# Last layer: the weights' low halves made by VectorE in thirds instead of by GpSimd in one piece

## The chip, the cores and the metric

One core of one Trainium2 chip runs the whole program. The metric is the time of one execution in microseconds (us) of device time. The engines are named as the profile names them: PE is TensorE (PEld its weight load), DVE is VectorE, ACT is ScalarE, POOL is GpSimd and SP is SyncE, which here only issues DMAs.

## The reference

Four layers follow each other on 8 x 512 tokens of 128 features. Only the last one is touched:

```python
x = x + layernorm(L1_ffn(layernorm(x)))

def L1_ffn(hidden, gate_W, w1_e, w3_e, w2_e, w1_s, w3_s, w2_s):    # 4096 tokens, 8 experts, F = 512
    probs = softmax(flat @ gate_W.T)
    top_v, top_i = top_k(probs, 2)
    gates = zeros(T, 8).at[arange(T)[:, None], top_i].set(top_v)
    g = silu(einsum('td,edf->etf', flat, w1_e))
    u = einsum('td,edf->etf', flat, w3_e)
    out_e = einsum('etf,efd->etd', g * u, w2_e)
    routed = einsum('te,etd->td', gates, out_e)
    shared = (the same silu(x w1_s) * (x w3_s) w2_s, summed over 8 slices of 64 features) / 8
    return 0.5 * shared + 0.5 * routed
```

Every token goes through the shared expert and through the two experts that the gate picked.

## The kernel before

The layer works in tiles of 512 tokens: 8 tiles of the shared expert first, then 23 tiles of routed tokens, which were scattered to DRAM by expert and are loaded one tile at a time. `TILES` lists the 31 tiles, and `uses[i]` is the weight set of tile i. The shared tiles use one set; every routed tile has its own set of three matrices (gate, up, down), each 128 x 512, loaded as one buffer `raw` of 128 x 3 x 512.

Products are made to near full precision from two halves: a number a is cut into a high half (fp32r, a copy rounded by ACT) and a low half a - high, and `mm3` (L108 to L110) adds three matmuls, high x high, high x low and low x high. So three kinds of operand are cut: the tokens of a tile (`xh`, `xl`), the weights (`wh`, `wl`) and the gated products of each step (`hh`, `hl`).

A tile has four steps c = 0 to 3, one for each 128 of the 512 hidden features; steps are counted through as m. In step m:

- PE: `up(m)`, three matmuls into a bank of `sw_g` and three into a bank of `sw_u`; then `down(m - 3)`, three into `sw_d`. At c = 0 it then turns the finished tile i - 2 back (`turn_out`, 4 transposes), at c = 1 it turns the next routed tile's tokens (`turn_in`, 4 transposes). `up` at c = 0 first waits until the tile's weights and tokens are cut: `wh_ready`, `wl_ready`, `xh_ready`, `xl_ready`. PE issues in this order alone, so what it waits for at `up` holds everything behind it.
- ACT: `gated(m)` (silu), `high_half(m - 1)` (`sw_hh`), at c = 1 `finish(i - 2)` (four `sw_yo` pieces), at c = 2 `token_high(i + 1)` (`sw_xh`), and at c = 0 `cut_high` of the next tile's weights (`sw_wh`, one instruction of 1536 columns).
- DVE: `product(m)` (`sw_hf`), `low_half(m - 1)` (`sw_hl`), at c = 2 `token_low(i + 1)` (`sw_xl`) behind these two, at c = 3 `fetch(i - 1)` (`sw_dT`).
- POOL: once a tile `cut_low` (`sw_wl`, 1536 columns) and `send(i - 2)`, four indirect stores of 128 tokens each into `sw_ys`. Before that, in the shared tiles, it issues 64 indirect stores that scatter the tokens (`scatter`).
- SP: loads of weights (two `raw` buffers, so a load waits until the set two before has been cut low) and of tokens (`xin`, five buffers).

The order on each engine is the order in which the code is written; nothing reorders it, and engines meet only at semaphores. For the first routed tile `turn_in` comes at c = 3, not at c = 1, so that the scatter can end first.

Of the kernel before, what the change touches and what calls it, by code (L numbers as in the profile page):

```python
# [6 lines left out]
F32 = mybir.dt.float32  # L7
# [3 lines left out]
ALU = mybir.AluOpType  # L11
ACT = mybir.ActivationFunctionType
# [9 lines left out]
FC = F // P  # L22
# [2482 lines left out]
def routed_layer(nc, X, ident, w, consts, out, padded):  # L2505
# [5 lines left out]
    XR, YR, RING, LAG, WR = 5, 3, 4, 3, 3  # L2511
    TILES = [("shared", b) for b in range(FRONT)] + [("routed", j) for j in range(NT)] + [("shared", b) for b in range(FRONT, B)]
    N = len(TILES)
# [8 lines left out]
    with ctx:  # L2522
# [73 lines left out]
        @block.sync  # L2596
        def _(sp):
            def load_weights(s, expert):
                if s >= 2:
                    sp.wait_ge(wl_ready, s - 1)  # L2600
                sp.dma_start(raw[s % 2][:], w["all"][expert]).then_inc(w_loaded[s % 2], 16)

            def store(b):
                sp.wait_ge(done, b + 1)
                sp.dma_start(out[b].rearrange("(t p) d -> p t d", p=P), X[:, b * T:(b + 1) * T, :]).then_inc(out_stored, 16)

            for dst, src in first_loads:
                sp.dma_start(dst, src).then_inc(first_loaded, 16)
            load_weights(0, NE)
            sp.dma_start(ids[:], consts["ids"]).then_inc(ids_loaded, 16)  # L2610
            for dst, src in table_loads:
                sp.dma_start(dst, src).then_inc(tables_loaded, 16)
            sp.wait_ge(where_ready, 1)
            for j in range(NT):
                expert = sp.value_load(where[0:1, 0, j:j + 1], min_val=0, max_val=NE - 1)
                load_weights(j + 1, expert)
                if j == 0:
                    sp.wait_ge(scattered, 16 * 2 * B * T)
                if j >= XR:
                    sp.wait_ge(y_stored[j % XR], 16 * T * (j // XR))  # L2620
                row = sp.value_load(where[0:1, 1, j:j + 1], min_val=0, max_val=NE * SEG)
                sp.dma_start(xin[j % XR][:], xs[bass.ds(row, S), :].rearrange("(c p) d -> p c d", p=P)).then_inc(x_loaded[j % XR], 16)
            if FRONT < B:
                load_weights(NT + 1, NE)
            for k in range(XR):
                sp.wait_ge(y_stored[k], 16 * T * len(range(k, NT, XR)))
            for b in range(B):
                pairs = ys[b * 2 * S:(b + 1) * 2 * S, :].rearrange("(p t k) d -> p t k d", t=T, k=2)
                sp.dma_start(chosen[b], pairs).then_inc(chosen_loaded[b], 16)
            for b in range(B):  # L2630
                store(b)
            sp.wait_ge(out_stored, B * 16)

        @block.tensor
        def _(pe):
# [38 lines left out]
            def up(m):  # L2674
                i, c = m // FC, m % FC
                if c == 0:
                    pe.wait_ge(wh_ready, uses[i] + 1)
                    pe.wait_ge(wl_ready, uses[i] + 1)
                    pe.wait_ge(xh_ready, i + 1)
                    pe.wait_ge(xl_ready, i + 1)  # L2680
                if m >= 2:
                    pe.wait_ge(silu_ready, m - 1)
                    pe.wait_ge(hf_ready, m - 1)
                tokens = (xh[i % 2][:], xl[i % 2][:])
                mm3(nc, g_bank[m % 2][:], both(uses[i], 0, c), tokens).then_inc(g_ps, 1)
                mm3(nc, u_bank[m % 2][:], both(uses[i], 1, c), tokens).then_inc(u_ps, 1)
# [63 lines left out]
        def _(act):  # L2750
# [8 lines left out]
                act.wait_ge(flip_ps, b + 1)  # L2759
                nc.scalar.activation(YT[:, b * S:(b + 1) * S], flips[b][:], ACT.Copy).then_inc(yT_ready, 1)  # L2760

            def cut_high(s):
                act.wait_ge(w_loaded[s % 2], 16 * (s // 2 + 1))
                if s >= WR:
                    act.wait_ge(d_used, FC * (last_use[s - WR] + 1))
                nc.scalar.activation(wh[s % WR][:], raw[s % 2][:], ACT.Copy).then_inc(wh_ready, 1)  # L2766

            def exponent(g):
                act.wait_ge(lg_ready, g + 1)
# [47 lines left out]
            for b in range(EARLY):  # L2817
                keep(b)
                if b == 0:
                    token_high(0)  # L2820
                if b + 2 <= EARLY:
                    normalise(b + 2)
                if b == 1:
                    cut_high(0)
            exponent(0)
            for m in range(M):
                i, c = m // FC, m % FC
                gated(m)
                if m >= 1:
                    high_half(m - 1)  # L2830
                if m == 1:
                    keep(EARLY)
                if 3 <= m < EARLY + 2:
                    keep(EARLY + m - 2)
                if 1 <= m < EARLY:
                    normalise(EARLY + m)
                if m == SHIFT:
                    exponent(1)
                if c == 1 and i >= 2:
                    finish(i - 2)  # L2840
                if i + 1 < N and c == min(turning(i + 1) + 1, FC - 1):
                    token_high(i + 1)
                if c == 0 and i + 1 < N and uses[i + 1] != uses[i]:
                    cut_high(uses[i + 1])
            high_half(M - 1)
            finish(N - 2)
            finish(N - 1)
# [4 lines left out]
        def _(pool):  # L2852
# [8 lines left out]
            def copy(b):  # L2861
                pool.wait_ge(y_ready, b + 1)
                nc.gpsimd.tensor_copy(rows[:, b * T:(b + 1) * T, 1, 0:D], rows[:, b * T:(b + 1) * T, 0, 0:D]).then_inc(copied, 1)

            def cut_low(s):
                pool.wait_ge(wh_ready, s + 1)
                nc.gpsimd.tensor_tensor(wl[s % WR][:], raw[s % 2][:], wh[s % WR][:].bitcast(F32), ALU.subtract).then_inc(wl_ready, 1)  # L2867

            def scatter(g):
                pool.wait_ge(slots_ready, g + 1)  # L2870
# [27 lines left out]
            for b in range(EARLY):  # L2898
                rsqrt(b + 1)
                copy(b)  # L2900
            cut_low(0)
            copy(EARLY)
            rsqrt(EARLY + 1)
            rsqrt(EARLY + 2)
# [2 lines left out]
            for g in range(G):  # L2907
                scatter(g)
            for i in range(FRONT - 1, N):
                if i + 1 < N and uses[i + 1] != uses[i]:  # L2910
                    cut_low(uses[i + 1])
                if i >= 2 and is_routed(i - 2):
                    send(i - 2)
            for i in (N - 2, N - 1):
# [9 lines left out]
        def _(dve):  # L2924
# [107 lines left out]
            def low_half(m):  # L3032
                dve.wait_ge(hh_ready, m + 1)
                if m >= RING:
                    dve.wait_ge(d_used, m - RING + 1)
                nc.vector.tensor_tensor(hl[m % RING][:], hf[m % 3][:], hh[m % RING][:].bitcast(F32), ALU.subtract).then_inc(hl_ready, 1)  # L3036

            def token_low(i):
                kind, n = TILES[i]
                dve.wait_ge(xh_ready, i + 1)  # L3040
                if i >= 2:
                    dve.wait_ge(u_ps, FC * (i - 1))
                src = t_in[:] if kind == "routed" else YT[:, n * S:(n + 1) * S]
                nc.vector.tensor_tensor(xl[i % 2][:], src, xh[i % 2][:].bitcast(F32), ALU.subtract).then_inc(xl_ready, 1)  # L3044
# [22 lines left out]
            for b in range(EARLY + 1):  # L3067
                input_moments(b + 1)
                offsets(b)
                if b == 0:  # L3070
                    dve.wait_ge(ids_loaded, 16)
                    nc.vector.tensor_copy(rows[:, :, :, D + 1].bitcast(U32), ids[:]).then_inc(ids_ready, 1)
                if b == 1:
                    dve.wait_ge(tables_loaded, 16 * len(table_loads))
                    for k, dst in enumerate((upper, before, same)):
                        nc.vector.tensor_copy(dst[:], tables[:, k, :]).then_inc(tables_ready, 1)
                if b == 2:
                    token_low(0)
            shift(0)
            dve.wait_ge(first_loaded, 16 * len(first_loads))  # L3080
            for _ in gate(0):
# [2 lines left out]
            for m in range(M):  # L3084
                i, c = m // FC, m % FC
                product(m)
                for _ in range(PER_STEP if m > SHIFT else 0):
                    next(later, None)
                if m >= 1:
                    low_half(m - 1)  # L3090
                for _ in range(PER_STEP if m > SHIFT else 0):
                    next(later, None)
                if m < EARLY - 1:
                    if EARLY + 2 + m < B:
                        input_moments(EARLY + 2 + m)
                    offsets(EARLY + 1 + m)
                if m == RANKS:
                    place(0)
                if m == SHIFT:
                    shift(1)  # L3100
                if m == LATER:
                    assert next(later, "none left") == "none left"
                    place(1)
                    plan()
                if i + 1 < N and c == min(turning(i + 1) + 1, FC - 1):
                    token_low(i + 1)
                if c == 3 and i >= 1:
                    fetch(i - 1)
            low_half(M - 1)
# [128 lines left out]
```

## Time and profile before

| | |
|---|---|
| three runs | 1780.53, 1784.54, 1786.31 us; median 1784.54 us |
| the profiled execution | 1779.97 us, of which the span of the trace is 1777.9 us |
| busy over the span | PE 1479.8 us (83%), DVE 1265.8 us (71%), ACT 1022.6 us (58%), POOL 826.4 us (46%) |
| the last layer | from about 1375 us; shared tiles 1390 to 1487 us, routed tiles 1500 to 1728 us, then the sums and the output |

A row of the timeline is one instruction (or several alike, merged): its start and its duration in us, the engine, the line, the operation, output and inputs, and in brackets how long its engine had been idle and who ended that. Two DVE or ACT instructions in a row overlap by some hundredths of a microsecond, so the distance of two starts is a little less than a duration. Matmul ends are modelled; the starts are what to go by.

### The profile page before, as it was taken

The page shows a single profiled execution, that of the slowest core. Times are in us where ns is not written, and L with a number is a line of the kernel's source. Part 1 is how long each engine was busy: PE and PEld are TensorE (multiplying, and loading weights), DVE is VectorE, ACT ScalarE, POOL GpSimd, SP SyncE. Part 2 cuts the span into 40 slices and gives each one's busy share as a digit, 9 for nine tenths or more (in the row PEclk, how much of TensorE's full clock was granted, in tenths as well). Part 3 has the DMA queues.
Part 4 walks back from the last instruction along what each step waited for, and adds up shares of the span by engine and source line. Part 5 has one row for each costly group of instructions (what it writes and reads, how often), then busy time and mean ns, then how long its engine had stood idle before and what let it go on. Part 6 is the DMA issues. An engine that isn't in the chain of part 4 may idle for free. (4 is left out here: it accounts for less than half of the span.)

```text
span 1777.9 us, 26868 instructions
## 1 busy us (share of the span) xinstructions
PE 1479.8 (83%) x8751; PEld 862.4 (49%) x8757; DVE 1265.8 (71%) x3276; ACT 1022.6 (58%) x1749; POOL 826.4 (46%) x935
## 2 busy tenths in 40 slices
PE   3788888679999999587769999999995787999980
PEld 1444455334444444333334555555552665777760
DVE  1656768568888886358677888878882574888875
ACT  2454555435666666235536777777775654777762
POOL 1244534555666654425731221222001575688875
PEclk8989989779999999689859999999998798999995
DMA  6800000222222221000434435454420023344414
GB/s 212 290 2 1 1 1 1 62 65 73 74 74 74 74 74 25 17 1 1 106 98 123 123 85 134 125 131 124 93 62 25 16 69 101 113 140 124 137 43 142
DMA packets 97225, 143.77 MB, mean 81 GB/s; under 512 B 31778, under 2 KB 64547, under 8 KB 94512
## 3 DMA queue, kind: packets, MB, share of 16 engines
q1 hardware_dynamic: 92096, 133.59, 26.8%
q0 software_dynamic: 4992, 8.48, 1.4%
q8 instruction: 71, 1.16, 0.3%
q14 instruction: 66, 0.54, 0.1%
HBM read 103.93 MB, written 57.22 MB: 91 GB/s over the span
## 5 line engine op out<-in xcount | busy, mean ns | idle before, releaser
L1259 DVE TENSOR_REDUCE ctx_nm<-ctx_s 128x1 f32<-128x512 f32 x496 | 325.1, 681 | 73.2 <-PE ctx_s L1415 72.0
L1259 DVE TENSOR_REDUCE rope_nm<-rope_s 128x1 f32<-128x128 f32 x496 | 221.1, 478 | 60.8 <-PE rope_s L1418 59.3
L1659 ACT ACTIVATE rope_probs<-rope_st 128x1024 f32<-128x1024 f32 (+1 forms) x256 | 171.2, 702 | 132.6 <-PE rope_st L1762 131.3
L1659 ACT ACTIVATE ctx_probs<-ctx_st 128x1024 f32<-128x1024 f32 x192 | 189.8, 1022 | 69.1 <-PE ctx_st L1762 64.9
L1415 PE MATMUL ctx_s<-att_kst,att_qst 96*128 96x512 f32 x496 | 209.4, 452 | 11.6 <-PEq L120 7.7
L1415 PE MATMUL rope_s<-att_kst,att_qst 96*128 96x128 bf16 x496 | 147.7, 313 | 31.3 <-DMA att_kst<-rope_halves 16.7
L1762 PE MATMUL ctx_st<-att_qst,att_kst 98*128 98x512 f32 x512 | 163.9, 403 | 0.0
L1415 PEld LDWEIGHTS ctx_s<-att_kst,att_qst 96*128 96x128 f32 x496 | 95.8, 193 | 124.9 <-issue 55.4
L1524 POOL TENSOR_SCALAR_AFFINE_SELECT rope_probs<-rope_probs 128x256 f32<-128x256 f32 x256 | 98.3, 411 | 106.9 <-ACT rope_probs L1659 106.6
L1778 PE MATMUL ctx_out<-ctx_probs,att_vaug 128*32 128x512 f32 x768 | 135.1, 604 | 0.0
L3036 DVE TENSOR_TENSOR sw_hl<-sw_hf,sw_hh 128x512 fp32r<-128x512 f32 x124 | 129.5, 1044 | 0.1
L3030 DVE TENSOR_TENSOR sw_hf<-sw_silu,sw_u 128x512 f32<-128x512 f32 x124 | 84.6, 682 | 62.4 <-ACT sw_silu L2788 60.6
L2788 ACT ACTIVATE sw_silu<-sw_g 128x512 f32<-128x512 f32 x124 | 74.3, 599 | 92.3 <-PE sw_g L110 91.8
L2888 POOL DMA_INDIRECT sw_ys<-sw_yo,sw_xin x92 | 104.2, 1133 | 29.1 <-issue 23.2
L1762 PE MATMUL rope_st<-att_qst,att_kst 98*128 98x512 bf16 (+3 forms) x512 | 114.0, 306 | 1.6 <-ACT rope_probs L1659 1.2
L1418 PE MATMUL rope_s<-rope_maskb,rope_identb 128*128 128x128 bf16 x496 | 111.6, 226 | 0.0
L1762 PEld LDWEIGHTS ctx_st<-att_qst,att_kst 98*128 98x128 f32 x512 | 97.8, 193 | 24.5 <-issue 4.6
L1778 PE MATMUL rope_out<-rope_probs,att_vaug 128*32 128x512 f32 (+3 forms) x1024 | 98.6, 459 | 7.9 <-POOL rope_probs L1524 7.9
L1415 PEld LDWEIGHTS rope_s<-att_kst,att_qst 96*128 96x128 bf16 x496 | 49.2, 99 | 113.8 <-DVE rope_nm L1259 57.6
L2867 POOL TENSOR_TENSOR sw_wl<-sw_raw,sw_wh 128x1536 fp32r<-128x1536 f32 x24 | 84.2, 3508 | 34.1 <-ACT sw_wh L2766 34.0
L2160 PE MATMUL mo_pb<-mo_we,mo_xT 128*128 128x512 f32 x128 | 73.4, 704 | 9.6 <-DVE mo_acc L2335 9.6
L2794 ACT ACTIVATE sw_hh<-sw_hf 128x512 fp32r<-128x512 f32 x124 | 77.3, 624 | 6.0 <-DVE sw_hf L3030 6.0
(440 smaller groups left out, 3461.5 us busy)
## 6 DMA issues: line engine op xcount, KB each, us to landing
sw_raw<-in_L_ffn_all SPq DMA_DIRECT2D x24, 768.0 KB, 4.5
sw_xs<-in_pad SPq DMA_DIRECT2D x65, 260.0 KB, 9.4
ctx_halves<-att_qk SPq DMA_DIRECT2D x24, 512.0 KB, 5.8
att_qst<-ctx_contexts SPq DMA_DIRECT2D x32, 384.0 KB
att_kst<-ctx_contexts SPq DMA_DIRECT2D x32, 384.0 KB
rope_halves<-att_qk SPq DMA_DIRECT2D x32, 256.0 KB, 3.4
att_qst<-rope_halves SPq DMA_DIRECT2D x32, 192.0 KB, 3.0
att_kst<-rope_halves SPq DMA_DIRECT2D x32, 192.0 KB, 3.3
```

The costliest lines, as they stand in the source:

```text
L1259: nc.vector.tensor_reduce(nm[:, g, j * T + t:j * T + t + 1], bank("s", b, n)[:, 0:keys], AXX, ALU.max, negate=True).then_inc(s_used, 1)
L1415: last = nc.tensor.matmul(out[:, 0:keys], qst[0:KS, g, j, t * P:(t + 1) * P], kst[0:KS, g, j, 0:keys], start=True, stop=not causal)
L1418: last = nc.tensor.matmul(out[:, keys - P:keys], identb[:], maskb[:], start=False, stop=True)
L1524: last = nc.gpsimd.affine_select(blocks, blocks, [[0, 2], [1, P]], compare_op=ALU.is_ge, fill=0.0, base=0, channel_multiplier=-1)
L1659: nc.scalar.activation(prob(n // GH % 2, n % GH)[:, u * units[0]:u * units[0] + units[u]], st_bank[u][:, 0:units[u]], ACT.Exp, scale=SCALE ...
L1762: last = nc.tensor.matmul(st_bank[u][:, lo:lo + width[c]], kst[:, g, j, c * P:(c + 1) * P], qst[:, g, j, S - width[c]:S], start=True, stop ...
L1778: last = nc.tensor.matmul(o_bank[32 * j:32 * j + 32, S - width[c]:S], vaug[g // 2][:, s, c, j, :], prob(s, j)[:, at(c):at(c) + width[c]], ...
L2794: nc.scalar.activation(hh[m % RING][:], hf[m % 3][:], ACT.Copy).then_inc(hh_ready, 1)
L2867: nc.gpsimd.tensor_tensor(wl[s % WR][:], raw[s % 2][:], wh[s % WR][:].bitcast(F32), ALU.subtract).then_inc(wl_ready, 1)
L2888: nc.gpsimd.indirect_dma_start(ys[:, :], bass.IndirectOffsetOnAxis(ap=where_to, axis=0), yo[j % YR][:, t, :], None, bounds_check=2 * B * S ...
L3030: nc.vector.tensor_tensor(hf[m % 3][:], silu[m % 2][:], u_bank[m % 2][:], ALU.mult).then_inc(hf_ready, 1)
L3036: nc.vector.tensor_tensor(hl[m % RING][:], hf[m % 3][:], hh[m % RING][:].bitcast(F32), ALU.subtract).then_inc(hl_ready, 1)
```

## The change

The low halves of the weights move from POOL to DVE, and both halves are made in thirds: one third is one of the three matrices, 512 columns. ACT makes third k of the next tile's set at the end of step c = k (k = 0, 1, 2); DVE makes the low third c - 1 in step c = 1, 2, 3, behind `low_half`. The waits count thirds. POOL keeps the indirect stores. `token_low` of the next tile moves ahead of `low_half` in its step. For the shared set, the three thirds are made before the first step.

```diff
             def load_weights(s, expert):
                 if s >= 2:
-                    sp.wait_ge(wl_ready, s - 1)
+                    sp.wait_ge(wl_ready, 3 * (s - 1))
...
                 if c == 0:
-                    pe.wait_ge(wh_ready, uses[i] + 1)
-                    pe.wait_ge(wl_ready, uses[i] + 1)
+                    pe.wait_ge(wh_ready, 3 * (uses[i] + 1))
+                    pe.wait_ge(wl_ready, 3 * (uses[i] + 1))
...
-            def cut_high(s):
+            def cut_high(s, k):
...
-                nc.scalar.activation(wh[s % WR][:], raw[s % 2][:], ACT.Copy).then_inc(wh_ready, 1)
+                nc.scalar.activation(wh[s % WR][:, k], raw[s % 2][:, k], ACT.Copy).then_inc(wh_ready, 1)
...
-                    cut_high(0)
+                    for k in range(3):
+                        cut_high(0, k)
...
-                if c == 0 and i + 1 < N and uses[i + 1] != uses[i]:
-                    cut_high(uses[i + 1])
+                if c < 3 and i + 1 < N and uses[i + 1] != uses[i]:
+                    cut_high(uses[i + 1], c)
...
-            def cut_low(s):
-                pool.wait_ge(wh_ready, s + 1)
-                nc.gpsimd.tensor_tensor(wl[s % WR][:], raw[s % 2][:], wh[s % WR][:].bitcast(F32), ALU.subtract).then_inc(wl_ready, 1)
...
-            cut_low(0)
...
-                if i + 1 < N and uses[i + 1] != uses[i]:
-                    cut_low(uses[i + 1])
...
+            def cut_low(s, k):
+                dve.wait_ge(wh_ready, 3 * s + k + 1)
+                nc.vector.tensor_tensor(wl[s % WR][:, k], raw[s % 2][:, k], wh[s % WR][:, k].bitcast(F32), ALU.subtract).then_inc(wl_ready, 1)
...
+            for k in range(3):
+                cut_low(0, k)
             shift(0)
...
                 product(m)
...
+                if i + 1 < N and c == min(turning(i + 1) + 1, FC - 1):
+                    token_low(i + 1)
                 if m >= 1:
                     low_half(m - 1)
+                if c >= 1 and i + 1 < N and uses[i + 1] != uses[i]:
+                    cut_low(uses[i + 1], c - 1)
...
-                if i + 1 < N and c == min(turning(i + 1) + 1, FC - 1):
-                    token_low(i + 1)
                 if c == 3 and i >= 1:
                     fetch(i - 1)
```

VectorE in steps 1, 2 and 3 of a routed tile, before (`sw_hf` product, `sw_hl` its low half, `sw_xl` the next tile's tokens, `sw_dT` the fetch):

```order
L3030 TENSOR_TENSOR sw_hf<-sw_silu,sw_u 128x512
L3036 TENSOR_TENSOR sw_hl<-sw_hf,sw_hh 128x512
L3030 TENSOR_TENSOR sw_hf<-sw_silu,sw_u 128x512
L3036 TENSOR_TENSOR sw_hl<-sw_hf,sw_hh 128x512
L3044 TENSOR_TENSOR sw_xl<-sw_t_in,sw_xh 128x512
L3030 TENSOR_TENSOR sw_hf<-sw_silu,sw_u 128x512
L3036 TENSOR_TENSOR sw_hl<-sw_hf,sw_hh 128x512
L3050 COPY sw_dT<-sw_d 128x512
```

Eight instructions, with `sw_xl` as the last of step 2. VectorE in the same three steps of the changed kernel (`sw_wl` is a low third; line numbers are the changed kernel's):

```order
L3024 TENSOR_TENSOR sw_hf<-sw_silu,sw_u 128x512
L3030 TENSOR_TENSOR sw_hl<-sw_hf,sw_hh 128x512
L3034 TENSOR_TENSOR sw_wl<-sw_raw,sw_wh 128x512
L3024 TENSOR_TENSOR sw_hf<-sw_silu,sw_u 128x512
L3042 TENSOR_TENSOR sw_xl<-sw_t_in,sw_xh 128x512
L3030 TENSOR_TENSOR sw_hl<-sw_hf,sw_hh 128x512
L3034 TENSOR_TENSOR sw_wl<-sw_raw,sw_wh 128x512
L3024 TENSOR_TENSOR sw_hf<-sw_silu,sw_u 128x512
L3030 TENSOR_TENSOR sw_hl<-sw_hf,sw_hh 128x512
L3034 TENSOR_TENSOR sw_wl<-sw_raw,sw_wh 128x512
L3048 COPY sw_dT<-sw_d 128x512
```

Eleven instructions; the last low third stands behind the product and the low half of step 3, and `sw_xl` stands between the product and the low half of step 2. ScalarE from the weights' copy of step 0 to step 3, before (`sw_silu` the gate, `sw_hh` the high half, `sw_yo` the finished tile, `sw_xh` the next tokens):

```order
L2766 ACTIVATE sw_wh<-sw_raw 128x1536
L2788 ACTIVATE sw_silu<-sw_g 128x512
L2794 ACTIVATE sw_hh<-sw_hf 128x512
L2805 ACTIVATE sw_yo<-sw_t_out,sw_xin 128x128 x4
L2788 ACTIVATE sw_silu<-sw_g 128x512
L2794 ACTIVATE sw_hh<-sw_hf 128x512
L2779 ACTIVATE sw_xh<-sw_t_in 128x512
L2788 ACTIVATE sw_silu<-sw_g 128x512
L2794 ACTIVATE sw_hh<-sw_hf 128x512
```

The copy is one instruction of 1536 columns. The same stretch of the changed kernel:

```order
L2766 ACTIVATE sw_wh<-sw_raw 128x512
L2788 ACTIVATE sw_silu<-sw_g 128x512
L2794 ACTIVATE sw_hh<-sw_hf 128x512
L2805 ACTIVATE sw_yo<-sw_t_out,sw_xin 128x128 x4
L2766 ACTIVATE sw_wh<-sw_raw 128x512
L2788 ACTIVATE sw_silu<-sw_g 128x512
L2794 ACTIVATE sw_hh<-sw_hf 128x512
L2779 ACTIVATE sw_xh<-sw_t_in 128x512
L2766 ACTIVATE sw_wh<-sw_raw 128x512
L2788 ACTIVATE sw_silu<-sw_g 128x512
L2794 ACTIVATE sw_hh<-sw_hf 128x512
```

Two of the three thirds now stand behind the work of steps 1 and 2.

## Rows read from the trace of the kernel before

**Rows 1.** Busy time by stretch: from:to, length, PE, PEld, DVE, ACT, POOL, clock, DMA.
```profile
1550.00:1575.00 25.00, 24.24 (x117) 19.40 (x117) 20.47 (x26) 19.39 (x37) 20.72 (x13) 1.00 0.41 130
```
**Rows 2.** Timeline of PE, one routed tile.
```profile
1559.54 0.47 PE L108 MATMUL sw_g<-sw_xh,sw_wh 128*128 128x512 f32 x1 [0.37 <-DVE sw_xl L3044]
...
1560.99 0.39 PE L108 MATMUL sw_d<-sw_hh,sw_wh 128*128 128x512 f32 x1
...
1562.81 0.40 PE L108 MATMUL sw_u<-sw_xh,sw_wh 128*128 128x512 f32 x1
...
1568.52 0.39 PE L110 MATMUL sw_d<-sw_hh,sw_wl 128*128 128x512 f32 x1
1569.30 0.47 PE L108 MATMUL sw_g<-sw_xh,sw_wh 128*128 128x512 f32 x1 [0.39 <-DVE sw_xl L3044]
```
**Rows 3.** Timeline of DVE, the same tile.
```profile
1561.85 0.69 DVE L3036 TENSOR_TENSOR sw_hl<-sw_hf,sw_hh 128x512 fp32r<-128x512 f32 x1
1563.76 0.69 DVE L3030 TENSOR_TENSOR sw_hf<-sw_silu,sw_u 128x512 f32<-128x512 f32 x1 [1.22 <-ACT sw_silu L2788]
1564.36 2.78 DVE L3036 TENSOR_TENSOR sw_hl<-sw_hf,sw_hh 128x512 fp32r<-128x512 f32 x1
...
1567.66 0.68 DVE L3036 TENSOR_TENSOR sw_hl<-sw_hf,sw_hh 128x512 fp32r<-128x512 f32 x1
1568.26 0.68 DVE L3044 TENSOR_TENSOR sw_xl<-sw_t_in,sw_xh 128x512 fp32r<-128x512 f32 x1
```
**Rows 4.** Timeline of POOL, the same tile.
```profile
1561.52 0.97 POOL L2888 DMA_INDIRECT sw_ys<-sw_yo,sw_xin  x1 [0.31 <-issue]
1563.08 3.50 POOL L2867 TENSOR_TENSOR sw_wl<-sw_raw,sw_wh 128x1536 fp32r<-128x1536 f32 x1 [0.59 <-ACT sw_wh L2766]
```
**Rows 5.** Groups by line, 1500 to 1728 us: count, busy us, mean ns, idle before.
```profile
L3036 DVE TENSOR_TENSOR sw_hl<-sw_hf,sw_hh 128x512 fp32r<-128x512 f32 x93 | 108.2, 1163 | 0.0
```
**Rows 6.** Timeline of ACT, the same tile.
```profile
1563.01 0.60 ACT L2788 ACTIVATE sw_silu<-sw_g 128x512 f32<-128x512 f32 x1
...
1564.02 1.14 ACT L2805 ACTIVATE sw_yo<-sw_t_out,sw_xin 128x128 f32<-128x128 f32 x4
1565.53 0.60 ACT L2788 ACTIVATE sw_silu<-sw_g 128x512 f32<-128x512 f32 x1 [0.37 <-PE sw_g L110]
1566.03 0.62 ACT L2794 ACTIVATE sw_hh<-sw_hf 128x512 fp32r<-128x512 f32 x1
1566.55 0.59 ACT L2779 ACTIVATE sw_xh<-sw_t_in 128x512 fp32r<-128x512 f32 x1
1567.59 0.60 ACT L2788 ACTIVATE sw_silu<-sw_g 128x512 f32<-128x512 f32 x1 [0.44 <-PE sw_g L110]
```
**Rows 7.** Timelines of DVE and PE at the first routed tile.
```profile
1498.73 0.69 DVE L3044 TENSOR_TENSOR sw_xl<-sw_t_in,sw_xh 128x512 fp32r<-128x512 f32 x1 [12.28 <-ACT sw_xh L2779]
...
1499.78 0.76 PE L108 MATMUL sw_g<-sw_xh,sw_wh 128*128 128x512 f32 x1 [1.78 <-DVE sw_xl L3044]
```
**Rows 8.** Timeline of DVE ahead of the first step.
```profile
1390.33 0.29 DVE L2977 TENSOR_REDUCE sw_red<-sw_d 128x16 f32<-128x128 f32 x1 [6.42 <-PE sw_d L2651]
```
**Rows 9.** Timeline of PE around two idle stretches.
```profile
417.47 0.23 PE L1415 MATMUL rope_s<-att_kst,att_qst 96*128 96x128 bf16 x1 [2.44 <-DMA att_kst<-rope_halves]
...
1433.97 0.47 PE L108 MATMUL sw_g<-sw_xh,sw_wh 128*128 128x512 f32 x1 [2.99 <-DVE sw_xl L3044]
...
1435.46 0.63 PE L108 MATMUL sw_d<-sw_hh,sw_wh 128*128 128x512 f32 x1
...
1438.85 0.40 PE L108 MATMUL sw_u<-sw_xh,sw_wh 128*128 128x512 f32 x1
```
**Rows 10.** Busy time by stretch around these two.
```profile
1431.00:1433.50 2.50, 0.00 (x0) 0.00 (x0) 2.40 (x8) 0.63 (x1) 1.90 (x2) 1.00 0.16 53
1436.00:1438.50 2.50, 2.50 (x10) 2.02 (x9) 1.45 (x3) 0.06 (x1) 1.89 (x3) 0.50 0.18 55
418.50:421.00 2.50, 2.50 (x13) 0.61 (x11) 2.50 (x12) 1.09 (x2) 0.77 (x2) 0.50 0.01 3
```

## The prediction

> **What bounds the kernel now.** I read the busy times by stretch first. In the routed tiles PE is busy 24.24 of 25 us at full clock, while DVE (20.47), ACT and POOL (20.72) have room [rows 1]. So the tile's length is PE's own work plus what PE waits. The timeline of PE gives both: one routed tile takes 9.76 us (1559.54 to 1569.30), and its only real stall stands in front of the next tile, where matmuls that otherwise start 0.23 us apart start 0.78 us apart, put down to `sw_xl` [rows 2]: 0.55 us a tile.
>
> Why `sw_xl` is late shows on DVE. A low half of 128 x 512 takes 0.68 us, and DVE starts such instructions 0.60 us apart (1567.66 to 1568.26), but once in every tile one takes 2.78 us: that of 1564.36 ends at 1567.14, 0.56 us after POOL's low half of the weights, which had begun first and ran from 1563.08 to 1566.58 [rows 3, 4]. The group's mean of 1163 ns against 0.68 is this one in four, 2.1 us a tile [rows 5]. What follows on DVE, `sw_xl` included, is late by it.
>
> The Trainium skill has a rule for this, "SBUF — State Buffer", section "Who interferes with whom": a VectorE instruction with two SBUF inputs and a GpSimd instruction that reads SBUF exclude each other, and the one that began first keeps the other out to its end. The trace agrees for POOL's subtraction; what the rule says of POOL's other work is a rival below.
>
> **The change part by part.** Times are counted from the first matmul of a routed tile, 1559.54.
>
> *POOL's 3.50 us go.* DVE gets back 2.1 us a tile, and on PE's path that is worth no more than the 0.55 us of the wait for `sw_xl`: 22 handovers between 23 routed tiles, 12 us. This is the gain that the change could have.
>
> *DVE's three thirds.* Each is a subtraction of the shape of `sw_hl`, so 0.68 us and 0.60 us of its queue: 1.8 us a tile against the 2.1 it gets back. By load the trade is even. By place it isn't: PE's `up` of the next tile waits for all three thirds, and the last stands in step 3, behind the product and the low half of that step.
>
> *The chain in step 2 and 3.* PE does the tile's own matmuls as before: the last one starts at 8.98 (1568.52), and the next tile could start 0.23 later, at 9.21. ACT in step 1 now makes a third behind `sw_yo`. That block ends at 5.62 (1564.02 + 1.14); with 0.52 for the third (the distance of `sw_hh` to `sw_xh`) ACT is free at about 6.1, and the silu of step 2, at 5.99 before, starts then [rows 6]. Now on:
> - silu at 6.1, `sw_hh` 0.50 later at 6.6, `sw_xh` at 7.1, which ends at 7.7 (0.59); the last third of the high half at 7.6; the silu of step 3 at 8.1 (8.05 before) [rows 6].
> - DVE's product of step 2 starts 0.75 after its silu (1563.01 to 1563.76) [rows 3, 6], so at 6.85, and is through at 7.45. `sw_xl`, which now comes next, must wait for the end of `sw_xh`: 7.73, with 0.03 for the semaphore. Then `sw_hl` at 8.33 and the second low third at 8.93.
> - The product of step 3 could start at 8.85 by its silu, but DVE is free at 9.53. So product 9.53, `sw_hl` 10.13, last third 10.73, ended at 11.41.
> - PE starts 0.36 after the end of what it waited for (`sw_xl` ends at 1499.42, PE at 1499.78) [rows 7]: 11.77.
>
> So the tile takes 11.77 instead of 9.76 us: 22 x 2.01 = 44.2 us. The stall for `sw_xl` goes; the one for `sw_wl` that takes its place is 2.56 us.
>
> *The clock.* PE's last matmul of a tile ends, as modelled, at 8.98 + 0.39 = 9.37, so the profile would show PE idle for 2.40 us in every tile. In this trace I find eleven idle stretches of PE of 2.4 to 4.2 us that began at full clock (2.4 GHz), and behind or within each the granted clock went to 0.5 (1.2 GHz). Two of them: after 2.99 us at 1433.97, clock 0.50 from about 1435.4; after 2.44 us at 417.47, 0.50 in the stretch from 418.5 [rows 9, 10]. Shorter ones did so in part. The price of one: at 1435.46 to 1438.85, 3.39 us, PE starts three matmuls of `down`, four transposes and three of `up`; at full clock the same ten take 1.82 (1560.99 to 1562.81) [rows 2, 9]. That is 1.57 us, and it falls into steps 0 and 1, where DVE waits for PE through ACT (1.22 us before the product) [rows 3] and nothing takes it up. 2.40 us lies at the short end of the eleven, so I take 19 of 22 handovers: 19 x 1.57 = 29.8 us. Bounds are none and all: 0 to 34.5.
>
> *Into the first routed tile.* There `token_low` waits for the scattered tokens, and the low half of the step before and the last third of the first set now stand behind it. So after `sw_xl` (1498.73) DVE has two more subtractions before PE may start: 2 x 0.60 = 1.2 us, once.
>
> *The rest costs nothing.* The shared set's thirds (1.8 us) go into the 6.42 us in which DVE waits for PE ahead of the first step [rows 8]; without that cover, 1.8. In the shared tiles, `sw_xl` ahead of `sw_hl` may free or hold PE by some tenths: 0, within 1 us either way. SP's loads of weights are released by the last third, some 2.5 us later in the tile than by POOL, and a set is cut two tiles after its load. POOL's four stores start about 1.5 us earlier. The end of the layer is not touched.
>
> **The sum**, from the profiled execution's own 1779.97: 44.2 + 29.8 + 1.2 = 75.2, so 1855. That execution lies 4.6 us under the median of the three runs shown and 0.6 under the fastest; I add half of the 4.6 and say 1857.
>
> **The rivals.**
> 1. *The clock holds.* 2.40 us is short of most of the eleven, and PE is busy around it. Then 44.2 + 1.2: 1825. For a clock that falls in up to ten tiles: up to 1841.
> 2. *DVE isn't late, only the order counts.* If `sw_xl` doesn't hold DVE, the product of step 3 starts at 8.85, the third ends at 10.73, PE starts at 11.1: 1.3 a tile, 29 us, and with 1.2 and a clock that holds at 1.8 us of stall: 1810. Against it: the row order puts the wait for `sw_xh` inside step 2 for certain.
> 3. *Faster: the last third is in time.* PE would start at 9.21 if the third ended by 8.85; then the 12 us of `sw_xl` are won and the time is 1768 (1771 with half of the 4.6). That is 2.56 us before I expect it, and before the product of step 3 alone can even begin. It would need a third of far less than 0.68 us, or a PE that runs ahead by something I don't see.
> 4. *POOL's stores hold the thirds up.* By the skill's rule above, a store that reads its row numbers from SBUF would keep out a subtraction as POOL's subtraction did. As a mechanism of this kernel: the stores now run at about 5.7 to 11.4 in the tile, beside the four subtractions of steps 2 and 3; each would lose about half a store's 0.97 us, 2 us a tile, 44 us more: 1901. The row speaks against it: the low half of 1561.85 took 0.69 us inside the store of 1561.52 to 1562.49 [rows 3, 4].
>
> **How the numbers follow.** The forecast (the clock falls in more than ten handovers, 1843 to 1868 with 0.3 us a tile either way) 0.62; rival 1 0.19; rival 2 0.08; rival 4 0.04; rival 3 0.05; no change 0.02. The range leaves out rival 3, rival 4 and the lower part of rival 2: 1815 to 1875. The forecast's own is 1843 to 1868. A difference of 0.3%, about 5 us, is the least that a measurement of this kernel can tell from none: faster 0.05, same 0.02, slower 0.93.
>
> **What would show it.** In the changed profile: PE's first matmul of a routed tile idle for about 2.4 us and put down to DVE `sw_wl`, not `sw_xl`; tiles 11.8 us long, or 13.4 where the clock fell; the granted clock of the routed stretch clearly under 1.00; every `sw_hl` at 0.68; DVE's last third begun about 10.7 us into the tile; on POOL the stores alone. It would be wrong if PE's wait at the handover were under 1 us, if `sw_wl` took much more or less than 0.68 us, or if the time came from outside 1500 to 1730 us of the layer.

## The result and the profile after

The changed kernel takes 1846.54 us (median of four runs, 1841.11 to 1848.74), the kernel before 1782.53 us beside it: a ratio of 1.035, 95% interval 1.032 to 1.039. It is slower by 64 us. The profiled execution took 1845.16 us with a span of 1843.4 us. Part 1 of its page (busy time, share of the span, instructions):

```profile
PE 1506.5 (82%) x8751; PEld 881.5 (48%) x8757; DVE 1265.2 (69%) x3348; ACT 1022.8 (55%) x1797; POOL 747.5 (41%) x911
```

POOL lost 79 us of work, and DVE took it over without being busier than before (1265.8 us). By the sums of these two engines the trade is free, as computed. Of the lost time only PE's 26.7 us more (1479.8 before) show here. Where it goes shows in the stretch of the routed tiles. Busy time by stretch, columns as in [rows 1]:

```profile
1520.00:1720.00 200.00, 166.60 (x701) 131.35 (x700) 130.02 (x208) 115.94 (x252) 73.48 (x60) 0.91 0.33 101
```

In the same 200 us the kernel before had PE busy for 191.91 us with 900 matmuls and a granted clock of 1.00. Now it is 166.60 us, 701 matmuls and 0.91. PE neither works all the time nor always at full clock. The timeline of PE over two tiles in a row, which answers to [rows 2]:

```profile
1579.86 0.47 PE L108 MATMUL sw_g<-sw_xh,sw_wh 128*128 128x512 f32 x1 [2.08 <-issue]
...
1581.67 0.63 PE L108 MATMUL sw_d<-sw_hh,sw_wh 128*128 128x512 f32 x1
...
1584.73 0.39 PE L108 MATMUL sw_u<-sw_xh,sw_wh 128*128 128x512 f32 x1
...
1590.44 0.39 PE L110 MATMUL sw_d<-sw_hh,sw_wl 128*128 128x512 f32 x1
1592.92 0.47 PE L108 MATMUL sw_g<-sw_xh,sw_wh 128*128 128x512 f32 x1 [2.10 <-issue]
...
1604.38 0.47 PE L108 MATMUL sw_g<-sw_xh,sw_wh 128*128 128x512 f32 x1 [2.10 <-issue]
```

Two tiles, and two lengths: 13.06 us (1579.86 to 1592.92) and 11.46 us (1592.92 to 1604.38), against 9.76 before. Both follow an idle stretch of 2.1 us. After the first of them the clock fell; after the second it did not. The granted clock (the number before the last two) in stretches around these handovers:

```profile
1577.50:1580.00 2.50, 0.42 (x3) 0.18 (x2) 2.50 (x5) 0.07 (x1) 2.20 (x2) 1.00 0.16 52
1580.00:1582.00 2.00, 2.00 (x7) 1.62 (x8) 0.38 (x2) 1.17 (x3) 0.61 (x1) 0.72 0.38 86
1582.00:1584.00 2.00, 2.00 (x8) 1.60 (x8) 1.26 (x2) 0.46 (x1) 0.00 (x0) 0.50 0.80 330
1592.50:1595.00 2.50, 2.08 (x9) 1.75 (x10) 1.30 (x3) 1.11 (x3) 1.18 (x1) 1.00 0.37 66
```

What PE waited for stands on DVE. The timeline of DVE for the end of the 13.06 us tile, which answers to [rows 3]:

```profile
1588.18 0.69 DVE L3024 TENSOR_TENSOR sw_hf<-sw_silu,sw_u 128x512 f32<-128x512 f32 x1 [0.62 <-ACT sw_silu L2788]
1589.13 0.69 DVE L3042 TENSOR_TENSOR sw_xl<-sw_t_in,sw_xh 128x512 fp32r<-128x512 f32 x1 [0.26 <-ACT sw_xh L2779]
1589.74 0.68 DVE L3030 TENSOR_TENSOR sw_hl<-sw_hf,sw_hh 128x512 fp32r<-128x512 f32 x1
1590.34 0.68 DVE L3034 TENSOR_TENSOR sw_wl<-sw_raw,sw_wh 128x512 fp32r<-128x512 f32 x1
1590.94 0.68 DVE L3024 TENSOR_TENSOR sw_hf<-sw_silu,sw_u 128x512 f32<-128x512 f32 x1
1591.54 0.68 DVE L3030 TENSOR_TENSOR sw_hl<-sw_hf,sw_hh 128x512 fp32r<-128x512 f32 x1
1592.14 0.68 DVE L3034 TENSOR_TENSOR sw_wl<-sw_raw,sw_wh 128x512 fp32r<-128x512 f32 x1
```

The long `sw_hl` of 2.78 us is gone; every subtraction takes 0.68 us. But from `sw_xl` on, six instructions of DVE's queue follow each other without a gap, and the last low third, the one thing that PE needs, is the last. It ends at 1592.82; PE starts at 1592.92. The profile itself names this releaser only once (2.7 us at the first routed tile). The other 22 stalls, 45.9 us, it puts down to "issue":

```profile
PE sw_g L108 <- issue: 45.9, 22, 2.1
```

(columns: total us, times, the longest). That PE starts 0.10 us behind the end of the third, in every tile, is the better witness, and the experiments move the two together.

**Where the 65.5 us of the span went.** The first step of the layer's tiles starts at 1394.10 instead of 1390.14: 4.0 us, from a part in which the change adds only the shared set's thirds. These take 1.90 us on DVE within its wait for PE, of which 3.75 us of the 6.42 are left [rows 8]. In the seven experiments it starts anywhere from 1383.8 to 1397.8, so this is the scatter of one execution. From there to the first routed tile it is 109.69 us instead of 109.64. The 22 distances from one routed tile's start to the next sum up to 277.2 us instead of 216.3: **+60.9 us**. What follows is longer by 0.6. So the whole effect lies in the routed tiles: one first distance of 13.97 us (11.02 before), seven near 11.48 and fourteen near 13.06 (9.77 before).

### The profile page after: what moved, and what is told of

Its sections match the earlier page's. It is cut to its first block and busy times, and to the rows that moved or that the text cites. A ratio compares the mean times of both kernels' runs of the same rounds, so it can differ in the third digit from the quotient of the medians.

```text
span 1843.4 us, 27006 instructions
## 1 busy us (share of the span) xinstructions
PE 1506.5 (82%) x8751; PEld 881.5 (48%) x8757; DVE 1265.2 (69%) x3348; ACT 1022.8 (55%) x1797; POOL 747.5 (41%) x911
## 5 line engine op out<-in xcount | busy, mean ns | idle before, releaser
L2885 POOL DMA_INDIRECT sw_ys<-sw_yo,sw_xin x92 | 110.3, 1199 | 200.3 <-ACT sw_yo L2805 178.2
L108 PE MATMUL sw_g<-sw_xh,sw_wh 128*128 128x512 f32 x124 | 60.1, 485 | 53.1 <-issue 45.9
L3030 DVE TENSOR_TENSOR sw_hl<-sw_hf,sw_hh 128x512 fp32r<-128x512 f32 x124 | 85.4, 689 | 0.1
```

The source lines that it names most:

```text
L108: nc.tensor.matmul(out, a[0], b[0], start=start, stop=False)
L2885: nc.gpsimd.indirect_dma_start(ys[:, :], bass.IndirectOffsetOnAxis(ap=where_to, axis=0), yo[j % YR][:, t, :], None, bounds_check=2 * B * S ...
```

## The experiments

Two theories of the stall stood against each other. *Place*: DVE has the time for the thirds, but the last one stands at the end of step 3. *Load*: DVE has too much to do beside PE. And of the rest: *clock*, the fall of the clock is a price of its own, caused by the stall. Times are medians; the kernel before took 1783.06 us beside the first four and 1781.62 us beside the last three. The tile column leaves out the first routed tile, and the clock is that of 1520 to 1720 us. The last column is the profiled span from the first step of the tiles to the end, which leaves out the scatter ahead of the layer.

| kernel | us | ratio to before, interval | routed tile, us | clock | from first step |
|---|---|---|---|---|---|
| before | 1783.06 and 1781.62 | 1 | 9.76 | 1.00 | 387.8 |
| after | 1846.54 | 1.035 (1.032 to 1.039) | 11.48 and 13.06 | 0.91 | 449.3 |
| e1_thirds_early | 1769.29 | 0.992 (0.989 to 0.995) | 9.10 to 9.15 | 1.00 | 372.8 |
| e2_tokens_alone | 1783.01 | 1.000 (0.997 to 1.002) | 9.71 to 9.76, two of 9.12 and 9.16 | 1.00 | 385.7 |
| e3_tokens_back | 1815.89 | 1.020 (1.017 to 1.023) | 11.12 to 11.16 | 1.00 | 418.1 |
| e4_pe_kept_busy | 1813.70 | 1.019 (1.016 to 1.022) | 11.42 to 11.50 | 1.00 | 426.8 |
| e5_last_in_step2 | 1778.47 | 0.998 (0.996 to 1.000) | 9.62 to 9.65 | 1.00 | 385.1 |
| e6_early_tokens_back | 1770.46 | 0.993 (0.991 to 0.996) | 9.09 to 9.15 | 1.00 | 372.8 |
| e7_two_thirds_pool | 1766.94 | 0.991 (0.988 to 0.993) | 9.10 to 9.15 | 1.00 | 373.2 |

### The same work, two steps earlier (e1_thirds_early)

From the changed kernel: ACT makes all three high thirds at the end of step 0, DVE two low thirds in step 0 and the last in step 1. There is not one instruction more or less.

```diff
-                if c < 3 and i + 1 < N and uses[i + 1] != uses[i]:
-                    cut_high(uses[i + 1], c)
+                if c == 0 and i + 1 < N and uses[i + 1] != uses[i]:
+                    for k in range(3):
+                        cut_high(uses[i + 1], k)
...
-                if c >= 1 and i + 1 < N and uses[i + 1] != uses[i]:
-                    cut_low(uses[i + 1], c - 1)
+                if i + 1 < N and uses[i + 1] != uses[i]:
+                    for k in ((0, 1), (2,), (), ())[c]:
+                        cut_low(uses[i + 1], k)
```

> The changed kernel with the same thirds on VectorE, made earlier: ScalarE makes all three in step 0, VectorE makes the first two in step 0 and the last in step 1. VectorE's work is the same, only its place differs. Place theory (the last third stood behind step 3's product): nothing holds PE at the handover, a routed tile is PE's own 9.1 to 9.2 us, 22 x 0.6 = 13 us under the kernel before: about 1769. Load theory (three more subtractions are too much for VectorE): no better than the kernel before, 1782 to 1846. PE's stall at the handover tells them apart: under 0.2 us or over 0.5.

Measured: 1769.29 us. DVE and PE of this kernel, one tile (its first matmul at 1578.99, the next tile's at 1588.09), from their timelines:

```profile
1581.81 1.29 DVE L3035 TENSOR_TENSOR sw_wl<-sw_raw,sw_wh 128x512 fp32r<-128x512 f32 x2
...
1584.32 0.69 DVE L3035 TENSOR_TENSOR sw_wl<-sw_raw,sw_wh 128x512 fp32r<-128x512 f32 x1
...
1586.53 0.69 DVE L3043 TENSOR_TENSOR sw_xl<-sw_t_in,sw_xh 128x512 fp32r<-128x512 f32 x1 [0.21 <-ACT sw_xh L2779]
```

```profile
1588.09 0.39 PE L108 MATMUL sw_g<-sw_xh,sw_wh 128*128 128x512 f32 x1
```

All three thirds are done 3 us before PE needs them, PE starts the next tile without a stall, and in 200 us it is busy for 198.53:

```profile
1520.00:1720.00 200.00, 198.53 (x957) 163.81 (x956) 175.26 (x279) 158.96 (x343) 83.90 (x85) 1.00 0.41 122
```

DVE does the same instructions and is now busier (175.26 us in the stretch), since more tiles go through. The load theory falls, the place theory stands. The tile's length of 9.12 us is PE's own work.

### Only the tokens moved (e2_tokens_alone)

From the kernel before: `token_low` ahead of `low_half`; POOL keeps the weights.

```diff
+                if i + 1 < N and c == min(turning(i + 1) + 1, FC - 1):
+                    token_low(i + 1)
                 if m >= 1:
                     low_half(m - 1)
...
-                if i + 1 < N and c == min(turning(i + 1) + 1, FC - 1):
-                    token_low(i + 1)
```

> The kernel before with one part of the change alone: token_low ahead of low_half; the weights' low half stays on GpSimd in one piece. Theory: sw_xl comes one subtraction (0.60 us) earlier, which covers the stall of 0.55 us, although the long sw_hl of 2.78 us stays; 22 x 0.55 = 12 us under the kernel before: about 1770. Rival (GpSimd's hold on VectorE must go for any gain, or GpSimd with about 9.1 us of work a tile becomes the bound): 1780 or more.

Measured: 1783.01 us, no difference from before; the gain that I leaned to is missed. Behind the first routed tile, two take 9.12 and 9.16 us, as the theory has it, and then it is 9.71 to 9.76. The timeline of POOL over one of the later tiles shows why:

```profile
1559.83 3.53 POOL L2867 TENSOR_TENSOR sw_wl<-sw_raw,sw_wh 128x1536 fp32r<-128x1536 f32 x1
1563.53 1.26 POOL L2888 DMA_INDIRECT sw_ys<-sw_yo,sw_xin  x1 [0.17 <-issue]
1565.09 1.47 POOL L2888 DMA_INDIRECT sw_ys<-sw_yo,sw_xin  x1 [0.30 <-issue]
1566.87 0.97 POOL L2888 DMA_INDIRECT sw_ys<-sw_yo,sw_xin  x1 [0.30 <-issue]
1568.14 1.42 POOL L2888 DMA_INDIRECT sw_ys<-sw_yo,sw_xin  x1 [0.30 <-issue]
1569.57 3.53 POOL L2867 TENSOR_TENSOR sw_wl<-sw_raw,sw_wh 128x1536 fp32r<-128x1536 f32 x1
```

POOL's round is 9.74 us (1559.83 to 1569.57), and the profile names nobody that it waits for: as soon as PE needs less than that, POOL is the bound. How that reaches PE stands on DVE and PE:

```profile
1560.58 3.33 DVE L3036 TENSOR_TENSOR sw_hl<-sw_hf,sw_hh 128x512 fp32r<-128x512 f32 x1
1563.84 0.68 DVE L3030 TENSOR_TENSOR sw_hf<-sw_silu,sw_u 128x512 f32<-128x512 f32 x1
1564.44 0.68 DVE L3044 TENSOR_TENSOR sw_xl<-sw_t_in,sw_xh 128x512 fp32r<-128x512 f32 x1
1565.04 0.68 DVE L3036 TENSOR_TENSOR sw_hl<-sw_hf,sw_hh 128x512 fp32r<-128x512 f32 x1
...
1568.03 0.68 DVE L3036 TENSOR_TENSOR sw_hl<-sw_hf,sw_hh 128x512 fp32r<-128x512 f32 x1
```

```profile
1565.48 0.47 PE L108 MATMUL sw_g<-sw_xh,sw_wh 128*128 128x512 f32 x1 [0.34 <-DVE sw_xl L3044]
```

POOL's subtraction begins 4.05 to 4.10 us into these tiles, where it was 3.45 and 3.50 in the two short ones, so it holds `sw_hl` for 3.33 us instead of 2.78, and `sw_xl` is late again in spite of its new place: PE waits for it at 19 handovers. So the 0.55 us in front of each tile of the kernel before [rows 2], which I had priced by the late `sw_xl` alone, had a second engine right behind it.

The stores are part of that. The three long ones began while a `sw_hl` was under way (it ended at 1563.91, 1565.72 and 1568.71) and ended 0.84 to 0.88 us after it; the one of 0.97 began with 0.05 us of another left. Every trace here shows the same. Of 828 stores in nine profiles, all 274 of more than 1.0 us began within a `sw_hl` or a `sw_wl` of DVE and ended 0.83 to 0.89 us after its end. None of the 461 that began outside one took more than 0.99 us, and neither did the other 93, nearly all of which began in the last 0.12 us of one. By this, 1.24 of POOL's 9.74 us are stores that VectorE's subtractions held up (5.12 us for four, against 4 x 0.97); no run tried that alone.

### Only the tokens moved back (e3_tokens_back)

From the changed kernel: `token_low` stands again at the end of step 2, so DVE does not wait for `sw_xh` in the middle of its queue. The thirds stay where the change put them.

```diff
-                if i + 1 < N and c == min(turning(i + 1) + 1, FC - 1):
-                    token_low(i + 1)
                 if m >= 1:
                     low_half(m - 1)
...
+                if i + 1 < N and c == min(turning(i + 1) + 1, FC - 1):
+                    token_low(i + 1)
```

> The changed kernel with token_low back at the end of step 2. Theory: VectorE no longer waits for sw_xh between product and low half, the last third ends at 11.0 us of the tile instead of 11.36, a tile at full clock takes 11.1 instead of 11.46; 22 x 0.36 = 8 us less, and PE's idle of about 1.75 us lets the clock fall more rarely: 1816 to 1838. If the order of token_low was the main harm: near 1782. If it plays no part: 1846.

Measured: 1815.89 us, just under the lower end of what was expected. The last third and the tile that waits for it, from the timelines of DVE and PE, and the busy time of the stretch:

```profile
1581.51 0.68 DVE L3034 TENSOR_TENSOR sw_wl<-sw_raw,sw_wh 128x512 fp32r<-128x512 f32 x1
```

```profile
1582.30 0.47 PE L108 MATMUL sw_g<-sw_xh,sw_wh 128*128 128x512 f32 x1 [1.75 <-DVE sw_wl L3034]
```

```profile
1520.00:1720.00 200.00, 168.44 (x790) 133.98 (x789) 144.96 (x234) 131.09 (x285) 77.59 (x68) 1.00 0.37 113
```

Two things follow. DVE's wait for `sw_xh` costs 0.32 us a tile (11.47 to 11.15): the move of `token_low` made the change worse, though it is the smaller part. And here the profile does name `sw_wl`: the same stall, shorter by 0.35 us, is no longer "issue". It is 1.74 to 1.77 us long in every tile, and the clock stayed at 1.00 throughout. So the 0.32 us removed the fall of the clock too: 449.3 - 418.1 = 31.2 us from the first step on, of which 22 x 0.32 = 7 are the wait itself; the rest is close to what the falls of the clock cost (below).

### The stall kept, PE kept busy (e4_pe_kept_busy)

From the changed kernel: nine matmuls whose result nobody reads fill PE's stall ahead of the wait for the weights. The wait for the last third stays as long as it was.

```diff
                 i, c = m // FC, m % FC
+                if c == 0 and i >= FRONT + 1:
+                    pe.wait_ge(xh_ready, i + 1)
+                    pe.wait_ge(xl_ready, i + 1)
+                    for _ in range(9):
+                        nc.tensor.matmul(t_in[:], xh[i % 2][:, 0:P], xh[i % 2][:], start=True, stop=True)
                 if c == 0:
```

> The changed kernel with nine matmuls without use (into the bank of sw_t_in, which is free by then) on PE ahead of its wait for the weights in each routed tile, about 2.05 us in which PE waited anyway. Clock theory (the long tiles of 13.06 us are those behind which the granted clock fell): granted clock 1.00, every tile about 11.5 us, 14 x 1.59 = 22 us less than the changed kernel: about 1824. If the long tiles have another cause: no change or longer, 1846 to 1860.

Measured: 1813.70 us, lower than expected. The timeline of PE at one handover, and the busy time of the stretch:

```profile
1585.73 2.20 PE L2680 MATMUL sw_t_in<-sw_xh 128*128 128x512 f32 x9
1588.01 0.47 PE L108 MATMUL sw_g<-sw_xh,sw_wh 128*128 128x512 f32 x1
```

```profile
1520.00:1720.00 200.00, 199.18 (x928) 159.76 (x927) 141.59 (x226) 128.70 (x282) 83.34 (x68) 1.00 0.37 113
```

The tiles are still 11.42 to 11.50 us long, so the stall is what it was; only the 13.06 us tiles are gone, and the clock is 1.00. From the first step on, it saves 449.3 - 426.8 = 22.5 us; fourteen falls at 13.06 - 11.47 = 1.59 us are 22.3. That shows the clock as a price of its own. The other 10 us by which this kernel beat its expectation lie ahead of the layer in the profiled execution (first step at 1383.79), where nothing was changed. There the granted clock was higher in this execution (0.82 between 700 and 950 us, 0.78 in the changed kernel's); why, and why the other three runs (1813.52 to 1818.89) are as short, stays open.

### The last third one step later (e5_last_in_step2)

As e1, with the thirds made in steps 0, 1 and 2.

```diff
-                    for k in ((0, 1), (2,), (), ())[c]:
+                    for k in ((0,), (1,), (2,), ())[c]:
```

> As e1, but VectorE makes one third in each of the steps 0, 1 and 2: each one step earlier than in the changed kernel, the last behind sw_xl and the low half of step 2. Theory (PE waits for the end of the last third, one for one): product of step 2 at 6.73 of the tile, sw_xl 7.63 (it waits for sw_xh), low half 8.23, third 8.83 to 9.51, PE 0.10 later at 9.61, so tiles of 9.6 us where e1 has 9.12: 22 x 0.5 = 11 us over e1, about 1780, clock 1.00. Rival (only the step behind the last product does harm): as e1, 1769.

Measured: 1778.47 us, tiles of 9.62 to 9.65. The last third from DVE's timeline and the handover from PE's:

```profile
1581.93 0.69 DVE L3035 TENSOR_TENSOR sw_wl<-sw_raw,sw_wh 128x512 fp32r<-128x512 f32 x1
```

```profile
1582.72 0.47 PE L108 MATMUL sw_g<-sw_xh,sw_wh 128*128 128x512 f32 x1 [0.24 <-issue]
```

The tile began at 1573.08 (9.64 us earlier), so the third ends 9.54 into it, 0.42 us after the 9.12 at which PE could go on, and PE starts 0.10 us later: 9.64. With e1, e3 and the changed kernel this makes four places of one instruction: the tile's length follows the end of the last third wherever that comes after PE's own 9.1 us, and not otherwise.

### Early thirds, tokens at the old place (e6_early_tokens_back)

e1 with `token_low` at the end of step 2, as e3 has it.

```diff
-                if i + 1 < N and c == min(turning(i + 1) + 1, FC - 1):
-                    token_low(i + 1)
                 if m >= 1:
                     low_half(m - 1)
...
+                if i + 1 < N and c == min(turning(i + 1) + 1, FC - 1):
+                    token_low(i + 1)
```

> As e1, with token_low back in its old place at the end of step 2. Theory: with the thirds out of the way, sw_xl ends at 8.62 of the tile at the latest, and with 0.36 to PE that is 8.98, before the 9.12 at which PE is ready: same as e1, 1769 within 4 us. If the new place of token_low is part of e1's gain: 0.3 us or more a tile over e1, 1776 or more.

Measured: 1770.46 us, 372.8 us from the first step on, as e1. Once the thirds are early, the place of `token_low` is worth nothing: there is room on both sides.

### POOL keeps two thirds (e7_two_thirds_pool)

e2, with the first third taken from POOL and made by DVE in step 1 (its own semaphore, which PE and SP wait for too).

```diff
-                nc.gpsimd.tensor_tensor(wl[s % WR][:], raw[s % 2][:], wh[s % WR][:].bitcast(F32), ALU.subtract).then_inc(wl_ready, 1)
+                nc.gpsimd.tensor_tensor(wl[s % WR][:, 1:3], raw[s % 2][:, 1:3], wh[s % WR][:, 1:3].bitcast(F32), ALU.subtract).then_inc(wl_ready, 1)
...
+            def cut_first(s):
+                dve.wait_ge(wh_ready, s + 1)
+                nc.vector.tensor_tensor(wl[s % WR][:, 0], raw[s % 2][:, 0], wh[s % WR][:, 0].bitcast(F32), ALU.subtract).then_inc(w1_ready, 1)
...
+                if c == 1 and i + 1 < N and uses[i + 1] != uses[i]:
+                    cut_first(uses[i + 1])
```

> As e2 (token_low ahead, GpSimd makes the low halves), but GpSimd makes two thirds and VectorE the first third in step 1. GpSimd's work a tile falls from the 9.74 us of e2 by about 1.17 to 8.6, and it still holds VectorE's sw_hl up, though for less. If e2 was bound by GpSimd's work: tiles of 9.12 us as in e1, about 1770. If the hold on VectorE is what costs: tiles over 9.4 us, 1776 or more.

Measured: 1766.94 us, tiles of 9.10 to 9.15. POOL and DVE of one tile, from their timelines:

```profile
1581.97 2.40 POOL L2869 TENSOR_TENSOR sw_wl<-sw_raw,sw_wh 128x1024 fp32r<-128x1024 f32 x1 [1.47 <-ACT sw_wh L2768]
1584.82 0.99 POOL L2890 DMA_INDIRECT sw_ys<-sw_yo,sw_xin  x1 [0.45 <-issue]
```

```profile
1583.24 1.67 DVE L3038 TENSOR_TENSOR sw_hl<-sw_hf,sw_hh 128x512 fp32r<-128x512 f32 x1
```

POOL waits for ACT again (1.47 us), so it no longer bounds the tile. One `sw_hl` is still held, 1.67 us instead of 0.68, and that costs nothing. So what limited e2 was POOL's round of 9.74 us; the hold on DVE was the way by which it reached PE. With `sw_xl` ahead the hold costs nothing by itself, here as in the two short tiles of e2 (a `sw_hl` of 2.78 us in tiles of 9.12 and 9.16). e1, e6 and e7 beat both kernels, by 11 to 15 us of the time before; their intervals overlap, and which of the three is fastest stays open.

## Why the prediction was right

Direction and mechanism came out, and the size nearly: 1857 us said, 1846.54 measured, within the forecast's own range of 1843 to 1868. Both large terms were too large, by 6.8 and 7.5 us. That the time still lies in the range is in part luck: 4.0 of the 65.5 us lie ahead of the first step and belong to no term, and without them the profiled execution would have taken about 1841. Point by point:

- **Load even, place late.** Right, and shown by e1: the same instructions in steps 0 and 1 make the kernel faster than before.
- **The chain of steps 2 and 3.** In the tile from 1592.92, the product of step 2 starts 6.73 us in, `sw_xl` 7.67, the last third 10.68, and it ends at 11.36 (said: 6.85, 7.73, 10.73 and 11.41). Timeline of DVE for two of these:

```profile
1599.65 0.69 DVE L3024 TENSOR_TENSOR sw_hf<-sw_silu,sw_u 128x512 f32<-128x512 f32 x1 [0.62 <-ACT sw_silu L2788]
1600.59 0.69 DVE L3042 TENSOR_TENSOR sw_xl<-sw_t_in,sw_xh 128x512 fp32r<-128x512 f32 x1 [0.26 <-ACT sw_xh L2779]
...
1603.60 0.68 DVE L3034 TENSOR_TENSOR sw_wl<-sw_raw,sw_wh 128x512 fp32r<-128x512 f32 x1
```

- **The handover**, mis-sized: I took 0.36 us from `sw_xl` to PE [rows 7]; from the last third to PE it is 0.10 us here, in e3 (0.11) and in e5. So a tile is longer by 1.70 us, not 2.01: 22 x 1.70 = 37.4 us for 44.2. PE's idle time is 2.06 to 2.12 us, not 2.40.
- **The clock**: the price was right (1.59 us for 1.57), the count was not: it fell at fourteen of the 21 handovers that a whole tile follows, and at the 22nd (0.54 between 1782.50 and 1786.00), whose tile has no next start to measure it by; I had 19 of 22. PE's idle time had come out 0.3 us shorter, and e3 shows that a still shorter one brings no fall. 14 x 1.59 = 22.3 us for 29.8. The first routed tile is 2.95 us longer, 1.70 of it the stall. The other 1.25 had not been in the sum, and that the change makes them is not shown: in every kernel the clock is low as this tile begins, behind PE's wait for the tokens, and its length varies with that (10.59 to 12.13 us in the four kernels with later tiles of 9.1 to 9.7).
- **Into the first routed tile**: from the end of `sw_xl` to PE it is 1.30 us instead of 0.36, so 0.94 us for the 1.2. The tokens arrive 0.9 us earlier after the first step than before, so of this nothing is left. The timelines of DVE and PE there, which answer to [rows 7]:

```profile
1501.80 0.69 DVE L3042 TENSOR_TENSOR sw_xl<-sw_t_in,sw_xh 128x512 fp32r<-128x512 f32 x1 [14.03 <-ACT sw_xh L2779]
1502.41 0.68 DVE L3030 TENSOR_TENSOR sw_hl<-sw_hf,sw_hh 128x512 fp32r<-128x512 f32 x1
1503.01 0.68 DVE L3034 TENSOR_TENSOR sw_wl<-sw_raw,sw_wh 128x512 fp32r<-128x512 f32 x1
```

```profile
1503.79 0.76 PE L108 MATMUL sw_g<-sw_xh,sw_wh 128*128 128x512 f32 x1 [2.72 <-DVE sw_wl L3034]
```

- **The gain that the change could have**, 12 us, put down to `sw_xl` alone: right in size for an early third (e1: 15 us from the first step on), incomplete in cause. In e2 `sw_xl` moves ahead and two tiles win the time; then POOL's round, as long as the tile, makes it late again. What the change had to offer was POOL's time, and it paid for it at the wrong place.
- **The rivals.** 1 (the clock holds) did not happen here, but it is what e4 makes of the kernel. 2 (`sw_xl` does not hold DVE) is what e3 makes of it: 11.15 us a tile for the 11.1 that it gave. 3 (the third in time) is e1. 4 did not happen. The whole group of the thirds (count, then shortest, median and longest in ns):

```profile
L3034 DVE TENSOR_TENSOR sw_wl<-sw_raw,sw_wh x72: 680/683/693, 1388.6 to 1780.2; 128x512 fp32r<-128x512 f32 x72
```

Not one of 72 is held up. Only two of them began inside a store, but with `sw_hl` that makes 42 subtractions, all of 0.68 or 0.69 us, and in e3 20 thirds did. It is the store that waits: of 92 here 42 began inside such a subtraction, and 41 of these took 1.31 to 1.50 us, the others 0.98 or 0.99. What the Trainium skill says ("SBUF — State Buffer", section "Who interferes with whom") of a GpSimd instruction that reads SBUF agrees with POOL's subtraction (`sw_hl` of 2.78 us before, of 1.67 us in e7). Of POOL's indirect stores it agrees one way only: a subtraction that began first keeps a store back, and a store that began first does not keep a subtraction back. The same section infers that generating a DMA's descriptors needs the write side of the shared port pair, where a subtraction of this kind takes the read side; by that alone no subtraction would hold a store up, and 41 stores were held up. The rival had read the rule too widely.

- **What would show it**: right, but for the releaser. I had said that the stall would be put down to `sw_wl`; the profile says "issue".

**Left open.** Why PE starts 0.10 us after a third's end and 0.36 us after the end of `sw_xl` was not tried. Nor was why the clock fell at some handovers and not at others behind the same idle time. The first step's 4 us were not tracked down, beyond that they vary as much among kernels that are alike there.

## What to carry to other kernels

Two engines can trade work that fits by sums and still lose, if the moved piece stands in an in-order queue behind work that is later than its deadline: write down the moment at which the consumer needs it and count the queue back from there. Here one list of steps, with the same instructions, is worth 77 us (1846.54 to 1769.29). A stall on PE has a second price, the granted clock, and that one can vanish with a few tenths of a microsecond; and before a late operand is moved, look whether another engine's round is already as long as the stage, or gets so once its work meets what was moved (e2: three of POOL's four stores held up).

## What was not expected of the hardware

- Idle stretches of PE of 2.06 to 2.12 us brought the granted clock from 2.4 to 1.2 GHz in fifteen of 22 handovers and left it alone in seven, with the same work around them. Of 1.74 to 1.77 us, in e3, none did. A fall costs 1.59 us.
- The profile's "issue" can stand for a wait: the same matmul starts 0.10 us after the last third in the changed kernel and in e5, where no releaser is named, and 0.11 in e3, where `sw_wl` is.
- POOL's subtraction holds VectorE's `sw_hl` up to 0.54 to 0.57 us past its own end: by 1 us for 1024 columns (e7), by 2.1 us for 1536 (before) and 2.65 (e2).
- POOL's indirect stores hold no subtraction of VectorE up (42 begun inside one: 0.68 or 0.69 us). The other way round it happens: a store that begins inside `sw_hl` or `sw_wl` ends 0.83 to 0.89 us after it, so that it takes up to 1.50 us instead of 0.97.
